# First units cut off one batch earlier, unit tables made before outputs, and unit rows requested by two engines

## The reference

```python
h = layernorm(x)                                   # (8, 100, 512)
x1 = h @ ctx.T                                     # (8, 100, 722)
x = x + (gelu_tanh(x1) * x1) @ ctx
t = layernorm(x).reshape(800, 512)
logits = t @ router_w                              # (800, 16)
e = argmax(logits); w = sigmoid(logits[e])
y = gelu(t @ w1[e] + b1[e]) @ w2[e] + b2[e]        # 512 -> 1024 -> 512
out = x + w * y
```

## Time and profile before

| | us |
|---|---|
| median of 3 runs | 325.29 (324.64 to 330.5) |
| profiled execution, its own time | 325.96 |
| its span, first to last instruction | 324.0 |
| TensorE busy | 252.4 (78%), 3,768 matmuls |
| VectorE busy | 115.2 (36%) |
| GpSimd busy | 68.1 (21%) |
| ScalarE busy | 32.4 (10%) |
| DMA | 100.11 MB, mean 309 GB/s |
| mean granted TensorE clock | 0.911 |

### The profile page before, as it was taken

One profiled execution on the slowest core, in us unless ns is written; L12 is line 12 of the kernel. 1 busy time (PEld: TensorE's weight loads), 2 busy tenths in 40 slices (PEclk: granted clock), 3 DMA queues, 4 the chain that ended last, 5 costly groups with the idle time before them and its releaser, 6 DMA issues.

```text
span 324.0 us, 10251 instructions
## 1 busy us (share of the span) xinstructions
PE 252.4 (78%) x3768; PEld 177.9 (55%) x3769; DVE 115.2 (36%) x387; ACT 32.4 (10%) x76; POOL 68.1 (21%) x110
## 2 busy tenths in 40 slices
PE   1899999999999399939564987878882967488860
PEld 0867867867867146616342755646561644355640
DVE  2144444444542253724311343433441322244420
ACT  1311112112101002100100001100110100011100
POOL 1001312312312412521201121231211121022221
PEclk9999999999999767989977899998996978599995
DMA  7999899999999993411699948999999889899500
GB/s 254 365 354 362 304 367 347 394 376 358 421 382 389 359 371 149 154 33 52 227 405 417 401 190 282 364 418 351 400 394 384 294 353 362 304 389 396 211 17 7
DMA packets 21289, 100.11 MB, mean 309 GB/s; under 512 B 3258, under 2 KB 7166, under 8 KB 12052
## 3 DMA queue, kind: packets, MB, share of 16 engines
q1 hardware_dynamic: 18692, 94.86, 78.2%
q0 software_dynamic: 2432, 4.69, 4.1%
q10 hardware_dynamic: 144, 0.27, 0.2%
HBM read 95.12 MB, written 5.14 MB: 309 GB/s over the span
## 4 chain that ended last, share of the span: by engine, by line
PE 55%; SPq 16%; issue 13%; DMA 6%; DVEq 4%; DVE 4%; POOL 0%; POOLq 0%
PE bank L405 15%; PE bank L325 12%; PE bank L332 11%; PE bank L394 8%; SPq L215 5%; SPq L265 5%; DMA rows<-row,pos 3%; PE bank L413 2%; DMA area<-rows 2%; DVE area L685 2%; DVEq L672 2%; PE bank L417 2%; PE bank L340 1%; SPq L271 1%; SPq L261 1%
## 5 line engine op out<-in xcount | busy, mean ns | idle before, releaser
L394 PE MATMUL bank<-W,area 128*32 128x256 f32 x1024 | 69.5, 416 | 18.7 <-issue 18.6
L405 PE MATMUL bank<-W,area 128*32 128x128 f32 x2048 | 70.9, 296 | 1.6 <-DVE area L717 1.5
L405 PEld LDWEIGHTS bank<-W,area 128*32 128x32 f32 x2048 | 60.8, 120 | 7.9 <-issue 2.2
L848 POOL DMA_INDIRECT out<-area,out_at x32 | 31.3, 979 | 134.9 <-DVE area L717 127.1
L394 PEld LDWEIGHTS bank<-W,area 128*32 128x32 f32 x1024 | 35.7, 118 | 43.1 <-issue 30.3
L325 PEld LDWEIGHTS bank<-xnT,area 128*128 128x128 f32 (+1 forms) x384 | 44.5, 193 | 4.7 <-issue 4.6
L332 PE MATMUL bank<-area,hidT 128*100 128x512 f32 (+1 forms) x96 | 46.8, 601 | 0.0
L325 PE MATMUL bank<-xnT,area 128*128 128x100 f32 (+1 forms) x384 | 44.9, 279 | 1.3 <-issue 1.3
L413 PE MATMUL bank<-con,area 128*128 128x128 f32 x33 | 11.1, 335 | 32.8 <-DVE area L685 32.5
L413 PEld LDWEIGHTS bank<-con,area 128*128 128x128 f32 x33 | 5.0, 152 | 47.7 <-issue 47.7
L504 ACT ACTIVATE area<-area 128x256 f32<-128x256 f32 x32 | 13.3, 416 | 173.9 <-PE bank L405 161.7
(11 more groups left out here) (85 smaller groups left out, 137.3 us busy)
## 6 DMA issues: line engine op xcount, KB each, us to landing
W<-in_w SPq DMA_DIRECT2D x64, 1024.0 KB, 11.6
area<-in_ctx_main SPq DMA_DIRECT2D x8, 1280.0 KB
area<-in_ctxT_a SPq DMA_DIRECT2D x8, 768.0 KB, 8.5
area<-in_ctxT_b SPq DMA_DIRECT2D x8, 676.0 KB, 7.7
area<-rows SPq DMA_DIRECT2D x28, 66.0 KB
xs<-in_x SPq DMA_DIRECT2D x8, 200.0 KB
area<-in_ctx_rest SPq DMA_DIRECT2D x8, 160.0 KB
out<-area,out_at POOLq DMA_INDIRECT x32, 5.6
```

The lines of the kernel that those rows point to most:

```text
L394: last = nc.tensor.matmul(p_h[U * q:U * q + U, 0:FQ], curT[:, U * k:U * k + U], mine, start=(k == 0), stop=(k == KD - 1), tile_position=(0 ...
L405: last = nc.tensor.matmul(p_y[U * q:U * q + U, 0:DQ], hT[:, U * c:U * c + U], W2[:, slot, c, DQ * q:DQ * q + DQ], start=(c == 0), stop=(c ...
L848: nc.gpsimd.indirect_dma_start(out_q, bass.IndirectOffsetOnAxis(ap=out_at[r][:, :], axis=0), y_out[:, r, :], None, bounds_check=last_out, ...
```

## The change

- `HEAD_END` is 5: the first units close after batch 4. GpSimd requests them at the start of its turn of batch 6, ahead of batch 5's scatter, and they go to a buffer of their own, `head`, outside the area that attention uses.
- `EARLY` issues 3 halves at batch 7 instead of 7; b2's load follows batch 7's products, and the 4 other halves follow it.
- TensorE runs batch 7's transposition, logits, ranks and counts before unit 1's first layer, with one b2 spread ahead of them; the other three spreads come between later layers. VectorE computes the unit tables (`units_of`) right after `pads`; they hold for each unit its expert (`eof`) and the block of `rows` that it begins at (`colof`), both turned to rows by TensorE.
- Rows are requested unit by unit from `colof` (`load_unit`). SyncE requests unit 4 after the scatters and the first pad, then units 5 to 7 and 8 to 13, ten in all; ScalarE requests 14 and 15, and after the gelu of each of units 3 to 7 three more, then what is left. Nothing of rows is left in SyncE's loop over weights. VectorE waits for groups: unit 4, 5 to 7, 8 to 13, 14 and 15, the rest. A fill by GpSimd marks unloaded units' outputs as unused.
- `biases` is split; `next_tokens(j+2)` stands right behind layer one's bias, ahead of `residual_bias` and `finish`.
- Two output buffers alternate to the end; a scatter of an unused one follows where the number of units is odd.

```diff
-HEAD_END = 6
+HEAD_END = 5
...
+BY_SP = 14
...
-EARLY = (0, 0, 1, 1, 1, 2, 4, 7)
+EARLY = (0, 0, 1, 1, 1, 2, 4, 3)
...
+        def load_unit(eng, j, signal):
+            at = bass.ds(j, 1) if not isinstance(j, int) else slice(j, j + 1)
+            col = eng.value_load(colof[0:1, at], min_val=0, max_val=E * PER - 1)
+            eng.dma_start(xr[:, at, :].rearrange("p o d -> p (o d)"),
+                          rows[bass.ds(col * U, U), :].rearrange("t (q d) -> q t d", q=Q)).then_inc(signal, 16)
...
-                if b == NB - 2:
-                    sp.wait_ge(s_x1ps[1], NB - 1)
+                if b == NB - 1:
+                    sp.wait_ge(s_x1ps[1], NB)
                     sp.dma_start(b2q.rearrange("q (e d) -> q e d", e=E),
                                  b2.rearrange("e (q d) -> q e d", q=Q)).then_inc(s_b2, 16)
...
+            load_weights(4 * SLOTS - sum(EARLY))
...
             sp.wait_ge(s_att, NB)
-            sp.wait_ge(s_b2ps, len(p_b2))
-            sp.wait_ge(s_plan, 1)
             for i in range(2):
                 sp.wait_ge(s_row[i], 16 * (NB // 2))
-            for e in range(SLOTS):
-                sp.wait_ge(s_pad[e // Q], 16)
-                load_rows(e, e, True)
-                if e > 0:
-                    rows_landed(e - 1, e - 1)
+            sp.wait_ge(s_pad[0], 16)
+            sp.dma_start(xr[:, SLOTS, :], rows[U:2 * U, :].rearrange("t (q d) -> q t d", q=Q)).then_inc(s_unit4, 16)
             for i in range(1, PADS):
                 sp.wait_ge(s_pad[i], 16)
+            sp.wait_ge(s_eof, 2)
+            with sp.Fori(SLOTS + 1, 8) as j:
+                load_unit(sp, j, s_near)
+            with sp.Fori(8, BY_SP) as j:
+                load_unit(sp, j, s_mid)
...
-                    load_rows(sp.snap(SLOTS * g + s), s, False)
...
-                    rows_landed(SLOTS * g + (s - 1), (s - 1) % SLOTS)
                     load_half(W1[:, s], first, s_w1[s], 0)
                     load_half(W1[:, s], first, s_w1[s], 1)
                     sp.wait_ge(s_y, before + 1)
-                    apart()
                     load_half(W2[:, s], second, s_w2[s], 0)
                     load_half(W2[:, s], second, s_w2[s], 1)
-            rows_landed(E - 1, SLOTS - 1)
...
 
             pe.sem_inc(s_y, 1)
             transpose_tokens(0)
+            transpose_x2(NB - 1)
+            first_layer(0, 0, 16)
+            transpose_tokens(1)
+            logits(NB - 1)
             pe.wait_ge(s_b2, 16)
             spread_b2(0)
-            first_layer(0, 0, 16)
-            transpose_x2(NB - 1)
-            transpose_tokens(1)
-            spread_b2(1)
-            logits(NB - 1)
-            first_layer(1, 1, 16)
             ranks(NB - 1)
             nc.tensor.matmul(p_lg[:, 0:E], ones, hot_sum[:, :], start=True, stop=False)
             nc.tensor.matmul(p_lg[:, 0:E], ones, hot[:, :], start=False, stop=True).then_inc(s_cntps, 1)
+            first_layer(1, 1, 16)
             transpose_tokens(2)
+            second_layer(0, 0, 16)
+            first_layer(2, 2, 16)
+            pe.wait_ge(s_tab, 10)
+            pe.wait_ge(s_pos, NB)
+            for i in range(2):
+                last = nc.tensor.transpose(p_rk[0:1, 64 * i:64 * i + MAXU], unit_f[:, i:i + 1], ident[0:MAXU, 0:MAXU])
+            last.then_inc(s_eofps, 1)
+            transpose_tokens(3)
+            second_layer(1, 1, 16)
+            spread_b2(1)
+            first_layer(3, 3, 16)
             spread_b2(2)
+            second_layer(2, 2, 16)
             pe.wait_ge(s_b2v, 1)
...
             nc.scalar.activation(warm[:, :], con[0:1, 0:1], ACT.Gelu)
             for j in range(3):
                 gelu_unit(j)
-            act.wait_ge(s_plan, 1)
+
+            act.wait_ge(s_eof, 2)
+            for i in range(2):
+                act.wait_ge(s_row[i], 16 * (NB // 2))
+            for i in range(PADS):
+                act.wait_ge(s_pad[i], 16)
+            act.wait_ge(s_blank, 1)
+            for j in range(BY_SP, BY_SP + 2):
+                load_unit(act, j, s_far)
             n = units(act)
-            with act.Fori(3, n) as j:
+            rest = act.value_load(n_less[0:1, 1:2], min_val=SLOTS + E - BY_SP - 3, max_val=MAXU - BY_SP - 3)
+            threes = act.snap(rest // 3)
+            with act.Fori(0, threes) as i:
+                gelu_unit(i + 3)
+                for k in range(3):
+                    load_unit(act, 3 * i + (BY_SP + 2 + k), s_rest)
+            with act.Fori(3 * threes + (BY_SP + 2), n) as j:
+                load_unit(act, j, s_rest)
+            with act.Fori(threes + 3, n) as j:
                 gelu_unit(j)
 
...
+                nc.vector.tensor_tensor(left[:, :], room_of, n_i[:, :], ALU.subtract).then_inc(s_tab, 1)
...
+                nc.vector.tensor_scalar(done[:, :], end_f[:, :], unit_no, None, ALU.is_le).then_inc(s_tab, 1)
+                dve.wait_ge(s_tab, 7)
+                nc.vector.tensor_tensor(room[:, :], done[:, :], left[:, :], ALU.mult).then_inc(s_tab, 1)
+                nc.vector.tensor_reduce(unit_f[:, 0:1], done[:, :], AX.X, ALU.add)
+                dve.wait_ge(s_tab, 8)
+                nc.vector.tensor_reduce(unit_f[:, 1:2], room[:, :], AX.X, ALU.add).then_inc(s_tab, 1)
+                dve.wait_ge(s_tab, 9)
+                nc.vector.tensor_scalar(unit_f[:, 1:2], unit_f[:, 1:2], unit_no, 1.0, ALU.add, ALU.add).then_inc(s_tab, 1)
+
+            def plan():
                 nc.vector.tensor_scalar(ends[:, :], end_f[0:1, :], float(SLOTS), None, ALU.add)
                 nc.vector.scalar_tensor_tensor(out=starts[:, :], in0=end_f[0:1, :], scalar=float(SLOTS), in1=n_i[0:1, :],
                                                op0=ALU.add, op1=ALU.subtract)
-                nc.vector.tensor_scalar(last_but_two[:, :], end_f[0:1, E - 1:E], float(SLOTS - 3), None, ALU.add)
-                nc.vector.tensor_scalar(last_unit[:, :], end_f[0:1, E - 1:E], float(SLOTS - 1), None, ALU.add)
-                dve.wait_ge(s_tab, 7)
-                nc.vector.tensor_scalar(slot_n[:, :], slot_f[:, :], 16.0, None, ALU.mult).then_inc(s_plan, 1)
-                nc.vector.tensor_scalar(done[:, :], end_f[:, :], unit_no, None, ALU.is_le).then_inc(s_tab, 1)
-                dve.wait_ge(s_tab, 8)
-                nc.vector.tensor_reduce(done_n[:, :], done[:, :], AX.X, ALU.add).then_inc(s_tab, 1)
-
-            def experts():
+                nc.vector.tensor_scalar(n_less[:, 0:1], end_f[0:1, E - 1:E], float(SLOTS - BY_SP - 2), None, ALU.add)
+                nc.vector.tensor_scalar(n_less[:, 1:2], end_f[0:1, E - 1:E], float(SLOTS - BY_SP - 3), None, ALU.add
+                                        ).then_inc(s_plan, 1)
+
+            def unit_tables():
                 dve.wait_ge(s_eofps, 1)
+                nc.vector.tensor_scalar(colof[:, :], p_rk[0:1, 64:64 + MAXU], 0.0, float(E * PER - 1), ALU.max, ALU.min
+                                        ).then_inc(s_eof, 1)
                 nc.vector.tensor_copy(eof[:, :], p_rk[0:1, 0:MAXU]).then_inc(s_eof, 1)
 
             def b2_copy(i):
...
-            def biases(j):
-                e = slice(j, j + 1) if isinstance(j, int) else bass.ds(expert_of(j), 1)
+            def hidden_bias(j, e):
...
+
+            def residual_bias(j, e):
...
-            b2_copy(0)
             next_tokens(1)
             hidden_units(0)
             tokens(1)
             dve.wait_ge(s_b1, 16)
-            dve.wait_ge(s_b2v, 1)
-            biases(0)
+            hidden_bias(0, expert_of(0))
             next_tokens(2)
-            b2_copy(1)
             route(NB - 1)
-            hidden_units(1)
             place(NB - 1)
             pads()
+            b2_copy(0)
+            units_of()
+            hidden_units(1)
             tokens(2)
-            biases(1)
+            hidden_bias(1, expert_of(1))
+            dve.wait_ge(s_b2v, 1)
+            residual_bias(0, expert_of(0))
             finish(0, 0)
             next_tokens(3)
             plan()
             hidden_units(2)
+            unit_tables()
             tokens(3)
-            biases(2)
-            experts()
+            hidden_bias(2, expert_of(2))
+            residual_bias(1, expert_of(1))
             finish(1, 1)
+            residual_bias(2, expert_of(2))
+            b2_copy(1)
+            next_tokens(4)
+            hidden_units(3)
 
             dve.wait_ge(s_xnps, NB)
             b2_copy(2)
+            tokens(4)
+            hidden_bias(3, expert_of(3))
+            dve.wait_ge(s_near, 16 * (7 - SLOTS))
+            next_tokens(5)
+            residual_bias(3, expert_of(3))
+            finish(2, 0)
             b2_copy(3)
-            next_tokens(4)
-            hidden_units(3)
-            tokens(4)
-            biases(3)
-            finish(2, 0)
-            dve.wait_ge(s_eof, 1)
+            dve.wait_ge(s_eof, 2)
             dve.wait_ge(s_b2v, len(p_b2))
-            last = dve.value_load(last_but_two[0:1, 0:1], min_val=SLOTS + E - 3, max_val=MAXU - 3)
-            next_tokens(5)
```

(73 more changed lines are left out.)

91 lines of the change are left out of this document (30 added, 61 removed).

## The result

The changed kernel takes 312.1 us (median of 4 runs, 309.75 to 313.52) where the kernel before takes 325.8 (4 runs on the same chip, 324.64 to 330.5). The ratio is 0.960, 95% interval 0.955 to 0.966. The direction of the prediction was right; the time was 17 us above its 295 and 4 above the upper end of its range. The profiled execution of the changed kernel is the fastest of the four, 309.75 us, with a span of 307.4, against 325.96 and 324.0 before.

The account below looks back on a forecast made before the run. The end was set by when the twelve-expert reload begins, how densely it runs and what follows: expert 7's weights at 183, plus 97.6, 3.5, 0.7 and 8.2 gives 293.0, with 1.96 outside the span 295 us; range 287 to 308.

Parts of the forecast that it names:

- Head at batch 4: First units' rows requested before batch 5's scatter: VectorE's 5.28 us wait goes, worth 4.9; late b2 gives 2 back.
- Plan ahead of the outputs: Spreads and first layers moved behind ranks and plan save 3 and 3; last rows scatter at 117.8 instead of 126.71.
- Rows by unit: SyncE's row requests at 2.0 each, from 127.5 for units 5 to 7; expert 4's weights at 146.5, 9.6 earlier.
- Units 5 to 11: First layer to first layer 41.3 as before, both TensorE stalls kept; unit 11's ends at 182.5, expert 7's weights at 183.
- rival 3: ScalarE's row requests, held by a full queue at 5.5 each, delay the gelus: end moves by 46 to 341; chance 0.04.
- The stream: Reload from expert 7 on, without row requests or landing waits: 37.7 MB at 395 GB/s, last weights landed at 280.6.
- Rival 1: Weight stream gets no denser, 194 to 304.5 keeps its 110.5: time 313, range 308 to 315; chance 0.15.
- The end: Last units end 3.5 after the last weights; last residual at 284.8, then 8.2 unchanged: span ends at 293.0.
- Rival 2: Fresh code on VectorE and ScalarE: two VectorE stalls between units 5 and 11 cost 8, giving 303; chance 0.12.
- Next tokens behind layer one's bias: Takes VectorE off the loop for transpositions of units 5, 10 and 11, some 0.5 each: a gain of 1.

Follow-up runs that it names:

- e_head6: The changed kernel with HEAD_END set back to 6, so the first units close after batch 5: 314.1 us, ratio 0.966 to the kernel before.
- e_pool: The changed kernel with GpSimd, not ScalarE, requesting the rows of units 14 to 31, after its output scatters: 297.9 us, ratio 0.917 to the kernel before.
- e_norest: The changed kernel without ScalarE's 16 requests for rows of units 16 to 31, whose output is left out: 292.8 us, ratio 0.896 to the kernel before.
- e_rows_back: The changed kernel plus 18 unawaited row requests by SyncE, one or two ahead of each expert's weights: 335.4 us, ratio 1.017 to the kernel before.
- e_next_late: The changed kernel with next tokens scaled behind the output step again, as before the change: 311.5 us, ratio 0.958 to the kernel before.

## Why the prediction was wrong, by its own steps

**Head at batch 4: right, and worth less than it seemed.** The first token scaling came at 106.75 (107 predicted). Two small waits took its place: batch 7's residual stood 1.25 for batch 5's scatter, and TensorE stood 2.10 for b2, which was priced at 2.

```profile
108.35 0.69 DVE L560 TENSOR_TENSOR row<-xs,bank 100x512 f32<-100x512 f32 x1 [1.25 <-DMA rows<-row,pos]
```

**Plan ahead of the outputs: right in kind, 2.9 short.** The last scatter of rows went at 120.68, not 117.8. (The prediction's next sum, 117.8 + 7.9, is 125.7 and not 125.5; nothing hangs on it.) The first layers of units 0 and 1 were priced at the full clock and ran at 3.18 and 3.39, and the spread still took 2.07: TensorE had stood for 1.54 and 2.10 just before them, and the clock granted over 107.3 to 116.3 was 0.79 on the mean. e_head6 shows in addition that hardly anything of the 4.9 counted for the head is in this sum: with the head closed later, the scatter moved by 0.7.

```profile
120.68 1.06 POOL L844 DMA_INDIRECT rows<-row,pos  x1 [9.15 <-DVE pad_at L637]
```

**Rows by unit: right in price, late in start.** Nine requests by SyncE took 17.60, 1.95 each, for which 2.0 was taken. They began at 132.12 instead of 127.5; the last pad's scatter, issued 5.3 behind the rows' and landing 4.9 later (median), is what the working left out. Expert 4's weights went at 151.03, not 146.5: the 2.9 from the step before, and 1.6 here.

**Units 5 to 11: the step that failed.** It said 41.3 from unit 5's first layer to unit 11's, "about 1" of it for ScalarE's requests at 2.0 each. Measured, it was 199.3 - 145.5 = 53.8. The 2.0 was right for the first eleven (1.8 in the bursts of 5.33 to 5.53). The burst at 152.16 was not held yet, though the first weights had been issued 1.1 before. The next, seven later, cost 20.78 for three, nearly 7 each; the gelu of unit 7 stood behind it, and TensorE 11.74 for the gelu. This is the mechanism of rival 3, which the prediction named and gave 4 in 100. It had the condition right (a request held by its queue) and dismissed it on two grounds that don't carry over. GpSimd's 0.7 is GpSimd's price: e_pool shows it under the full DMA while ScalarE's rose to 8.9. And that ScalarE's queue holds only small requests is no help where these go out at 13 packets per us and are asked for at 74. Rival 3 was itself wrong in extent: not fifteen requests were held but a few of the last seven, so the loss was 19 and not the 46 that would have decided against the change.

**The same step had a second error that hid.** Without the requests, e_norest took 180.1 - 145.6 = 34.5 and not 41.3: one break of 4.19 where two, of 5.36 and 4.06, were kept from the earlier trace rows, which is 5.2 of the 6.8; the other 1.6 were not traced. That is why e_norest's 180.1 lies near the predicted 182.5 although unit 5's first layer ended 4.4 later than predicted (145.6 for 141.2): two errors that nearly cancel.

**The stream: right, rather too cautious.** It was taken at 395 GB/s; it ran at 403 over the whole of 199.5 to 290, at 420 and more in the page's steady slices. Rival 1 (no denser) is refuted. The reason given was half right: scaled from e_rows_back, about 17 of the 23 us are due to the row requests between the weights and not to SyncE's waits.

**The end: right.** From expert 7's weights to the end 110.0 were predicted, 107.9 measured. The last residual waited for TensorE alone:

```profile
299.65 0.35 DVE L732 SCALAR_TENSOR_TENSOR area<-bank,area 128x128 f32 x1 [2.20 <-PE bank L401]
```

**Rival 2** is not borne out as priced: of VectorE's new stands one at the loop of unit 6 may be its own (1.9 in e_norest and 2.9 in the changed kernel behind the data, or else the wait for rows), where it asked for two worth 8. The breaks of about 4 us stayed on TensorE. The DMA view speaks for code fetches there: of the queue of kind "instruction" one packet of 0.02 MB falls within the break of the changed kernel (161.5 to 165.4), none within its 11.74 us:

```profile
q8 instruction: 1, 0.02, 1.8%
```

The same holds for both breaks of the kernel before (158.7 to 164.0 and 170.9 to 174.9). One such packet also stands at 149 to 150, within VectorE's stand, but SyncE enters new code there too. The view doesn't say for which engine a packet is, and no run took the fetches away, so the cause of the breaks stays argued. **Next tokens behind layer one's bias** was counted as a gain of 1; e_next_late shows none that can be measured.

As a sum in span times: unit 5's first layer +4.3, the requests under the full DMA +19.3 (53.8 - 34.5), fewer breaks and what was not traced -6.8 (34.5 - 41.3), and the part behind unit 11's first layer -2.4 (108.1 - 110.5). 293.0 + 14.4 = 307.4, the span measured.
